# Four transfers and norms in another order in a two-layer decoder kernel

## What is computed

```python
x = x + L0_attn(layernorm(x), ...)            # 32 heads, 8 key/value heads, rope, sink
x = x + L0_xattn(layernorm(x), mask, ctx)     # own keys plus keys of ctx, tanh gate
x = x + L0_ffn(layernorm(x), ...)             # 8 experts, each row goes to 2 of them
x = x + L1_attn(layernorm(x), Wq, Wk_down, Wk_up, Wv_down, Wv_up, ..., Wo)   # 16 heads, causal
x = x + L1_xattn(layernorm(x), ctx, mask)     # one head over ctx
x = x + L1_ffn(layernorm(x), ...)             # amplitude, phase, two entangling layers
```

## Time and profile before

| | |
|---|---|
| median of 3 runs | 1948.1 us (1944.89 to 1949.48) |
| the profiled execution | 1944.75 us |
| its span | 1942.9 us |
| its mean granted PE clock | 0.975 |
| PE busy | 1827.4 us (94%) |
| DVE busy | 1009.9 us (52%) |
| ACT busy | 604.6 us (31%) |
| POOL busy | 392.4 us (20%) |
| instructions | 29167 |

### The profile page before, as it was taken

The page is one execution under the profiler, slowest core; times in us unless marked ns, Lnnn a source line. Parts: engine busy times, 40 slices in busy tenths (PEclk is TensorE's granted clock), DMA queues, the critical chain, the costliest instruction groups (busy, mean ns, idle before and its releaser), DMA issues.

```text
span 1942.9 us, 29167 instructions
## 1 busy us (share of the span) xinstructions
PE 1827.4 (94%) x11802; PEld 1202.3 (62%) x11802; DVE 1009.9 (52%) x1860; ACT 604.6 (31%) x1931; POOL 392.4 (20%) x456
## 2 busy tenths in 40 slices
PE   6899999999999999999898999987899999999798
PEld 5766666645665665665564888857576574444344
DVE  3665556425656666566733111126444454574799
ACT  0223222315555555555630101100311212232411
POOL 3432223410110110110003000015021120000588
PEclk9999999999999999999888999998999999999999
DMA  9000002000000000000226888872000030642011
GB/s 382 22 1 1 1 1 103 1 16 31 2 17 17 1 17 17 2 17 2 109 105 225 331 324 342 337 257 86 1 1 1 1 117 33 245 154 116 1 38 38
DMA packets 30965, 170.70 MB, mean 88 GB/s; under 512 B 3848, under 2 KB 3848, under 8 KB 17168
## 3 DMA queue, kind: packets, MB, share of 16 engines
q1 hardware_dynamic: 28272, 161.50, 22.2%
q0 software_dynamic: 2560, 7.34, 1.2%
HBM read 155.98 MB, written 16.52 MB: 89 GB/s over the span
## 4 chain that ended last, share of the span: by engine, by line
PE 78%; DVE 9%; issue 4%; POOL 4%; ACT 2%; DMA 2%; SPq 0%; POOLq 0%; DVEq 0%; ACTq 0%
PE PS L1145 8%; PE PS L1225 6%; PE PS L982 6%; PE PS L933 6%; PE PS L1185 5%; PE PS L1022 4%; PE PS L1013 4%; PE PS L1061 4%; PE PS L1154 4%; PE PS L1258 3%; PE PS L1045 3%; PE PS L990 2%; PE PS L1081 2%; PE PS L1216 1%; PE PS L1054 1%
## 5 line engine op out<-in xcount | busy, mean ns | idle before, releaser
L2048 POOL TENSOR_TENSOR rstd<-veps,mhalf 112x1 f32<-112x1 f32 (+1 forms) x76 | 57.6, 758 | 601.6 <-DVE veps L1318 587.2
L1145 PEld LDWEIGHTS PS<-R,W 128*128 128x128 f32 x1344 | 156.0, 195 | 11.9 <-issue 11.9
L1145 PE MATMUL PS<-R,W 128*128 128x128 f32 x1344 | 156.4, 278 | 2.2 <-DVE R L1615 2.2
L1444 DVE TENSOR_REDUCE nmx<-PS 112x2 f32<-112x750 f32 x128 | 114.0, 932 | 84.5 <-PE PS L1045 84.5
L1910 ACT ACTIVATE R<-PS,nmx 112x375 f32<-112x375 f32 x256 | 142.9, 573 | 0.8 <-DVE nmx L1444 0.8
L1389 DVE TENSOR_TENSOR x<-x,PS 112x512 f32<-112x512 f32 x40 | 27.5, 687 | 195.7 <-PE PS L1225 93.8
L933 PE MATMUL PS<-xT,W 128*128 128x224 f32 x640 | 125.1, 356 | 0.0
L933 PEld LDWEIGHTS PS<-xT,W 128*128 128x128 f32 x640 | 122.1, 192 | 4.8 <-issue 4.4
L1622 DVE TENSOR_TENSOR R<-R,PS 128x512 f32<-128x512 f32 x21 | 14.4, 688 | 201.9 <-PE PS L1145 201.9
L1258 PE MATMUL PS<-W 128*128 128x512 f32 x256 | 118.5, 606 | 0.0
L1225 PE MATMUL PS<-W,R 128*112 128x512 f32 x256 | 116.0, 607 | 0.8 <-DVE R L1674 0.8
(11 more groups left out here) (292 smaller groups left out, 3284.8 us busy)
## 6 DMA issues: line engine op xcount, KB each, us to landing
W<-in_we SPq DMA_DIRECT2D x63, 1024.0 KB, 7.6
W<-in_entwT SPq DMA_DIRECT2D x8, 1024.0 KB, 7.0
W<-in_entpw SPq DMA_DIRECT2D x8, 1024.0 KB, 8.6
W<-in_ctxT SPq DMA_DIRECT2D x8, 750.0 KB, 4.3
R<-in_ctxT SPq DMA_DIRECT2D x8, 750.0 KB, 8.1
R<-in_ctx SPq DMA_DIRECT2D x8, 750.0 KB
xs_rows<-in_x SPq DMA_DIRECT2D x3, 1792.0 KB, 39.0
R<-xs_rows SPq DMA_DIRECT2D x21, 256.0 KB, 8.2
```

Of the source, the lines that this page charges most:

```text
L1145: o = e.matmul(PS[:, m, c * 128:(c + 1) * 128], gate_up(j % 3, k, off + c * 128), BT[:, j % 2, k, :], start=k == 0, stop=k == 3)
L1444: e.tensor_reduce(nmx[0:S, par, r:r + 2], PS[0:S, r:r + 2, 0:SC], AX.X, ALU.max, negate=True).then_inc(*up("cmax", (b, c, par, r)))
```

## The change

Four things are put in another order. No product, copy or transfer is added or taken away.

1. In `cross`, for batch 0 alone, the first half of the norms and projections of the next pair of batches is laid before the keys and values of batch 1's context, and not behind them. In even batches after the first the order is as it was.
2. In `experts`, the loads before the first block are `experts`, `rows 0`, `we 1`, `rows 1`, `rows 2`, `we 2`, where they were `we 1`, `experts`, `rows 0`, `rows 1`, `rows 2`, `we 2`.
3. The loads of `w1q 2` and of `w1o` leave the end of `experts`. `w1q 2` stands before the first `mix` and waits in addition until the gather of batch 3 has landed; the four `w1o` stand behind the query products of the first pair and wait until the gather of batch 7 has landed. The load of `mu` follows them.
4. The steps `stats` and `scale` of batches 2 and 3 of stage 3 stand behind `mix(5)`, and their `turn` behind `mix(6)`, within the query products; `mix(4)` to `mix(7)` stand at places written out by hand.

```diff
-            fill, nxt = fill + nxt[:len(nxt) // 2], nxt[len(nxt) // 2:]
+            first, nxt = nxt[:len(nxt) // 2], nxt[len(nxt) // 2:]
+            fill = fill + first if b else first + fill
...
-    out += [("load", "we", 1), ("load", "experts", 0)] + [("load", "rows", j) for j in range(3)] + [("load", "we", 2)]
+    out += [("load", "experts", 0), ("load", "rows", 0), ("load", "we", 1), ("load", "rows", 1), ("load", "rows", 2), ("load", "we", 2)]
...
-    out += [("load", "w1q", 2), ("load", "w1o", 2), ("load", "w1o", 3), ("load", "w1o", 0), ("load", "w1o", 1)]
     out += part(range(FRONT, 16)) + [("wc", 0, 0), ("wc", 0, 2)]
...
-    out += [("load", "mu", 0)] + [("mix", 0), ("get", 4), ("mix", 1), ("get", 5)] + rows(3, (0, 1)) + [("mix", 2), ("get", 6), ("mix", 3), ("get", 7)] + project1(0)[:6]
-    out += spread(project1(0)[6:], [("mix", b) for b in range(4, NBATCH)], lambda s: 1.0)
-    out += rows(3, (2, 3))
+    out += [("load", "w1q", 2)] + [("mix", 0), ("get", 4), ("mix", 1), ("get", 5)] + rows(3, (0, 1)) + [("mix", 2), ("get", 6), ("mix", 3), ("get", 7)] + project1(0)[:6]
+    kq = project1(0)[6:]
+    out += kq[:1] + [("mix", 4)] + kq[1:2] + [("mix", 5)] + norms(3, (2, 3)) + kq[2:4] + [("mix", 6)] + turns(3, (2, 3)) + kq[4:5]
+    out += [("mix", 7)] + kq[5:] + [("load", "w1o", n) for n in (2, 3, 0, 1)] + [("load", "mu", 0)]
...
                     w.wait_ge(*(at("upped", NBLK - 2), at("expert", NBLK - 2), at("upped", NBLK - 1), at("expert", NBLK - 3))[n])
+                    if n == 2:
+                        w.wait_ge(*at("d_get3", (3, 1)))
...
                 elif what == "w1o":
+                    w.wait_ge(*at("d_get3", (7, 1)))
                     if n >= 2:
```

## The result

| | before | after |
|---|---|---|
| median of the first runs (3 each) | 1948.1 us (1944.89 to 1949.48) | 1930.85 us (1929.05 to 1931.52) |
| ratio, 95% interval | | 0.9914 [0.9895, 0.9934] |
| the changed kernel timed again, with more runs of before (6; 17) | 1945.39 us | 1931.15 us, ratio 0.9933 [0.9918, 0.9949] |
| the profiled execution | 1944.75 us | 1931.52 us |
| its span, mean granted clock | 1942.9 us, 0.975 | 1929.6 us, 0.980 |

The change made the kernel faster by 17.3 us by the first medians, and by 14.2 us by the larger sets.

The account below looks back on a forecast made before the run. PE, busy 94% of the span with 78% of the chain, was taken as the bound, so only its waits and low clock count. 1.5 + 3.7 + 1.4 + 1.8 = 8.4 us off 1948.1 gave 1939.7, range 1933.5 to 1945.5.

Parts of the forecast that it names:

- the four waits: PE's waits: context keys 4.0 us, first block's rows 6.3, normed rows 10.6 and 3.9; each a queue's order, not work.
- Part A: Cross attention, batch 0: later keys hide the context load, a 3.0 us bank wait appears; gain 1.5 us.
- its clock term: Cross attention: 1.6 us more lost if the clock falls after the new bank wait; gain 2.8 or 1.2.
- Part B: Experts, first block: rows before block 1's weights; 3.0 from landing, 1.2 from clock, 0.5 charged for rows; gain 3.7 us.
- the puts keep their share beside the weights: Experts: if engines take turns between queues, the 3.0 us landing gain is about nothing; total near 1943.4, chance 0.04.
- The rival of rows 0 sharing the engines: Experts: rows 0 share engines with later loads and land at 1069.5, losing 15.2 us; 1958.6 us, chance 0.04.
- Part C: Between experts and layer 1: weights behind the gathers let the first mix start 1.4 us earlier, bounds 1.0 and 1.7.
- Part D: Layer 1: norms inside the query projections gain 2.5 us, limited by VectorE's queue, less 0.7 for clock: 1.8 us.
- The sum: Whole kernel: 1.5 + 3.7 + 1.4 + 1.8 = 8.4 us faster.
- The forecast's clock terms: Low clock after pauses: 1.2 us taken back at first `gu`, 0.7 charged before softmax transposes, gain 1.5 chosen between 2.8 and 1.2.
- The base: Whole kernel: start from the runs' median of 1948.1 us, 3.3 above the profiled execution's 1944.75.
- Rival (2): Clock stays up in cross attention and at `gu(0)`: 13.7 us faster, 1934.4 us, chance 0.14.

Follow-up runs that it names:

- A alone: Kernel before with only the reordering of cross attention's fill in batch 0: 1942.77 us, ratio 0.9989.
- shift by ten: Ten extra products with unread results near 60 us: on the changed kernel 1935.52 us, ratio 0.9953; on the kernel before 1951.24 us, ratio 1.0026.
- two orders: Changed kernel with norms of batches 4 and 5 behind the first softmax's first half, and the last expert block's sums behind four mixes: 1930.48 us, ratio 0.9922.
- B alone: Kernel before with only the new order of loads ahead of the first expert block: 1940.42 us, ratio 0.9976.
- The run with the norms moved: Changed kernel with the norms of batches 4 and 5 laid in VectorE's queue behind the first softmax's first half: 1928.1 us, ratio 0.9911.
- C and D: Kernel before with both the weight and mask loads behind the gathers and the norms and turns within the query projections: 1937.76 us, ratio 0.9968.
- unread products: Changed kernel with 20 extra products, results unread, laid where PE would wait at three places: 1928.39 us, ratio to before 0.9913.
- D alone: Kernel before with only the norms and turns of batches 2 and 3 laid into the query projections: 1944.6 us, ratio 0.9995.
- shift by four on the kernel before: Kernel before with four extra products, results unread, before one query product near 60 us: 1947.48 us, ratio 1.0015.

## Why the prediction was right and wrong

- **What bounds the kernel, and that the four waits are queues' orders: right.** Each wait went where the text sent it.
- **Part A: mechanism right, its clock term wrong.** Norms forecast at 3.6 took 3.9; the maxima began at 444.5 (forecast 443.7) and PE waited 2.95 us (3.0). I took off 1.6 for a low clock, since 2.85 us had lowered it; it didn't fall in the changed kernel, nor with A alone. Gain 2.5 in place of 1.5. Of the nine profiles with this wait, seven had the full clock behind it and two, the shift by ten and the two orders, a low stretch of 3.4 us, worth 1.7: both values of the forecast exist, and the profile of before couldn't tell which.
- **Part B: right in sum, 4.0 for 3.7, by other terms, so the sum is partly luck.** The landing gave 3.35 and the whole idleness 3.5 (3.0); rows 1 were not late (0.5 charged); of the low clock 0.5 came back, not 1.2, because the stretch ended 5.6 us after the first `gu` began, and 5.8 us after it before: what was cut from its length lay ahead of the work. In the second profile 1.8 came back there, and the stages of part B gave 3.6 in all, for a longer low stretch stood ahead of the wait. The Trainium skill has the DMA engines take turns between queues ("DMA: Bandwidth & Descriptors", section "Queues, rings and completion order"). What I drew from that, that the puts keep their share beside the weights, is wrong for this load: they landed in 3.0 us instead of 7.5, and the last one in 2.96 with B alone too. Whether the engines take turns, no row shows. The rival of rows 0 sharing the engines fell too: they landed in 2.60 us with block 1's 3 MB and more issued behind them.
- **Part C: right at its place, nearly half lost behind it.** The turn came 1.2 us earlier (1.4 forecast); 0.5 of it was lost to the low clock in `td`, which lasts from 1302 to 1316 here, and 0.7 is left. The text kept the length of the rest of the way, which for the clock was not so.
- **Part D: right, 2.1 for 1.8.** The products and turns grew by 2.0 (0.9 and 1.0 forecast), and the transposes came 11.9 us behind the scores' start, from 1353.3 to 1365.2 in the forecast's own terms: 11.9. The run with the norms moved bears out the queue named.
- **The sum: the failed step.** It took the rest of the kernel as fixed. The stages of the parts gave 9.3 us where 8.4 were forecast; 4.6 us came from low stretches behind pauses of 1.3 to 2 us that the change does not touch, at 1393, 1434 and 1639. The forecast's clock terms came to under a microsecond (0.2 in A, 1.2 in B, -0.7 in D), and 8.4 of the 13.3 us between the profiles are the clock's. I had read the rows of low clock only where the change works. The text granted that a low stretch may follow a pause, and not that it may vanish behind one that stays. Why it vanished stays open.
- **The base: the second failed step.** The forecast started from 1948.1, the median of three runs, 3.3 above the profiled run. Sets of 31, 17, 19 and 13 runs of the same kernel gave 1944.82, 1945.39, 1946.03 and 1945.49. From 1945.4 the 8.4 us would have led to 1937.0, and the truth lies 5.9 below that; the median had added some 3 us to the miss, and I had allowed one microsecond of scatter.
- **Rival (2), the clock staying up, was nearest in size (13.7 us) and half right in kind:** it stayed up in A, and at `gu(0)` it didn't, or in part. It knew nothing of the three stretches, so its nearness in size is luck.

## What to carry to other kernels

An order's gain is what its own stage shows, plus or minus what the clock does at every later pause; where a kernel has many pauses of one to three microseconds, list all its low stretches first, count what they cost (some 38 us here), and widen the range by a few of them (1.7 us each) to both sides. Take the base from as many runs as there are, and when it stands 3 us off the profiled run, put that into the range as well. Where pauses are short, two edits can together give what neither gives alone, as C and D did here: test them alone and together before one is thrown away.

## What the runs showed of the hardware that I had not expected

- Low-clock stretches were 3.4, 6.8, 10.2, 13.7 or 17.1 us long, but for the one that the end of the span cuts. The 17 profiles held 12 to 18 of them each, 58 (unread products) to 109 us (D alone) in all, and 23 to 40 us were lost in them.
- One pause of 1.33 us, of equal length in 17 profiles, had a low stretch behind it in eight and none in nine. A wait of 2.95 us had one in two profiles (shift by ten on the changed kernel, two orders) and none in seven.
- 1.5 us of products at 60 us changed which stretches stood 1330 us later (shift by four on the kernel before).
- An fp32 product leaves two records in the trace: ten added ones are x20, of 0.19 us each from start to start (shift by ten), so a product of 128x224 takes 0.38 us.
- Executions of one kernel scattered by up to 15.7 us (with D alone, 1936.82 to 1952.51), more than any of the four parts is worth.
